# An output projection's bias: from a two-row product on the matrix engine to an add on GpSimd, in a fused embedding, state-space and mixture-of-experts kernel

## The reference

```python
def _L0_attn_ref(x, ...):
    ...                                            # u: projections, gate, convolution
    _, ys = jax.lax.scan(step, init, ...)          # state-space recurrence
    y = jnp.transpose(ys, (1, 0, 2))
    out = jnp.einsum('blh,dh->bld', y, W_out) + b_out
    return _layernorm(x + out, ln_g, ln_b)
...
h = tokens                                          # embedding of patches and text
h = h + _L0_attn_ref(_layernorm(h), ...)
h = h + _L0_ffn_ref(_layernorm(h), ...)             # router, top 2 of 4 experts, combined
```

## Time and profile before

| | us |
|---|---|
| three runs | 497.41, 498.78, 499.92 |
| median | 498.78 |
| span of the profiled execution, first to last instruction | 495.2 |
| busy in it: PE, DVE, ACT, POOL | 442.5, 330.5, 296.4, 152.2 |

### The profile page before, as it was taken

The page is one execution under the profiler, slowest core; times in us unless marked ns, Lnnn a source line. Parts: engine busy times, 40 slices in busy tenths (PEclk is TensorE's granted clock), DMA queues, the critical chain, the costliest instruction groups (busy, mean ns, idle before and its releaser), DMA issues.

```text
span 495.2 us, 9980 instructions
## 1 busy us (share of the span) xinstructions
PE 442.5 (89%) x3149; PEld 363.4 (73%) x3149; DVE 330.5 (67%) x980; ACT 296.4 (60%) x667; POOL 152.2 (31%) x255
## 2 busy tenths in 40 slices
PE   8989989799899999999999798999999999999400
PEld 5769967667778878887777577888878888888300
DVE  6885567678999434335786777866674666666584
ACT  2854359177975465316554354887786777877341
POOL 2000000000000000001243887874778644543322
PEclk9999999799999999999999999999999999999955
DMA  7981089900019942972511222232322333252262
GB/s 178 187 228 56 33 253 322 292 0 2 1 35 259 217 114 58 228 228 81 180 54 52 89 94 77 86 97 66 107 98 76 107 107 110 74 155 69 78 213 82
DMA packets 58734, 59.94 MB, mean 121 GB/s; under 512 B 25368, under 2 KB 51260, under 8 KB 57404
## 3 DMA queue, kind: packets, MB, share of 16 engines
q1 hardware_dynamic: 54236, 48.68, 36.4%
q0 software_dynamic: 3552, 9.74, 5.3%
q10 hardware_dynamic: 896, 0.89, 0.6%
HBM read 34.50 MB, written 24.80 MB: 120 GB/s over the span
## 4 chain that ended last, share of the span: by engine, by line
PE 66%; DVE 12%; issue 7%; ACT 7%; POOL 4%; DMA 2%; SPq 1%; DVEq 0%; POOLq 0%; ACTq 0%
PE bank L1040 14%; PE bank L881 9%; PE bank L433 8%; PE bank L435 8%; PE bank L434 8%; PE bank L955 3%; PE bank L1030 3%; PE bank L901 3%; POOL sorted_x L671 2%; PE bank L1012 2%; ACT U L470 1%; DVE spj L1400 1%; DMA got<-expert_y 1%; PE bank L848 1%; PE bank L947 1%
## 5 line engine op out<-in xcount | busy, mean ns | idle before, releaser
L1040 PE MATMUL bank<-w,hr 128*128 x320 | 76.0, 380 | 1.5 <-DVE ysb L1661 1.5
L1040 PEld LDWEIGHTS bank<-w,hr 128*128 128x128 f32 x320 | 60.1, 190 | 11.7 <-issue 2.7
L644 POOL MEMSET ones<- 2x128 f32 x1 | 0.2, 194 | 212.3 <-PE bank L916 212.3
L1234 ACT ACTIVATE hr<-bank,gsel 128x128 f32<-128x128 f32 x160 | 59.9, 460 | 0.2 <-PE bank L1030 0.2
L719 POOL DMA_INDIRECT expert_y<-ysb,toid x40 | 42.8, 1071 | 51.3 <-DVE ysb L1661 34.7
L881 PE MATMUL bank<-Tb,U 68*32 68x68 f32 x1024 | 45.9, 358 | 0.3 <-issue 0.3
L881 PEld LDWEIGHTS bank<-Tb,U 68*32 68x32 f32 x1024 | 40.6, 139 | 3.6 <-issue 3.1
L1646 DVE BATCH_NORM_STATS2 bsth<-bank 128x6 f32<-128x512 f32 x40 | 27.7, 693 | 20.5 <-PE bank L435 20.2
L671 POOL DMA_INDIRECT sorted_x<-x2s,slot x34 | 33.8, 994 | 15.3 <-issue 9.2
L1226 ACT ACTIVATE hn<-bank,nmrh,rsh 128x512 f32<-128x512 f32 x40 | 31.1, 777 | 10.0 <-DVE nmrh L1655 8.1
L433 PE MATMUL bank<-w_hi,bT_hi 128*128 x80 | 35.0, 438 | 0.1
(11 more groups left out here) (297 smaller groups left out, 1153.3 us busy)
## 6 DMA issues: line engine op xcount, KB each, us to landing
Tb<-ssm_kernels SPq DMA_DIRECT2D x16, 680.0 KB, 7.5
sorted_x<-zpad SPq DMA_DIRECT2D x6, 1419.0 KB, 13.6
xg<-sorted_x SPq DMA_DIRECT2D x40, 129.0 KB, 2.1
got<-expert_y SPq DMA_DIRECT2D x17, 256.0 KB, 3.6
XI<-in_x_dram SPq DMA_DIRECT2D x12, 288.0 KB, 5.6
h0r<-h_spill SPq DMA_DIRECT2D x17, 128.0 KB, 2.1
out_dram<-acc SPq DMA_DIRECT2D x17, 128.0 KB
w1raw<-in_L_ffn_w_dram SPq DMA_DIRECT2D x4, 512.0 KB, 15.9
```

The source lines that it names most:

```text
L1040: mm = pe.matmul(bank[6][:, 0:D], hr[:, i % 3, c, :], w2[:, bass.ds(expert[i], 1), c, :].rearrange("p o n -> p (o n)"), start=(c == 0), st ...
L1234: last = act.activation(hr[:, i % 3, c, :], bank[3 + i % 2][:, c * P:(c + 1) * P], ACT.Relu, scale=gsel[:, i, 0, c:c + 1], bias=gsel[:, i, ...
```

## The change

The bias is no longer a product. One DMA brings it to all 128 partitions (`bo`), POOL adds it to `xb` in the step `h0b`, ahead of the add that was there, and DVE's sum waits for POOL's semaphore `xb_bias` instead of ACT's `xb`. The product L959, its operands and the instructions that made them are gone. The planned times and so the order of steps on each engine are as before.

```diff
-        bo = zjunk[0:2, 1, :]
+        bo = zjunk[:, 1, :]
...
-                    for n in range(2):
-                        sp.dma_start(bo[n:n + 1, :], ins["L0_attn_b_out"].rearrange("(o d) -> o d", o=1)).then_inc(sem("small_in"), 16)
+                    sp.dma_start(bo, ins["L0_attn_b_out"].partition_broadcast(P)).then_inc(sem("small_in"), 16)
...
                 if kind == "h0b":
                     pool.wait_ge(sem("xb"), i + 1)
-                    pool.wait_ge(sem("small_in"), 80)
+                    pool.wait_ge(sem("small_in"), 144)
+                    pool.tensor_tensor(xb[:, i % 3, :], xb[:, i % 3, :], bo, ALU.add).then_inc(sem("xb_bias"), 1)
                     pool.tensor_tensor(h0r[:, i % 4, :], h0r[:, i % 4, :], lnb_b[:], ALU.add).then_inc(sem("h0b"), 1)
...
                     for j in range(HC):
-                        pe.matmul(ps, yT[:, i % 2, j, :], Wo[:, j, :], start=(j == 0), stop=False)
-                    if i == 0:
-                        pe.wait_ge(sem("router"), 2 + 2 * DC)
-                        pe.wait_ge(sem("block_consts"), 1)
-                    pe.matmul(ps, ones2[:], bo_hl[:], start=False, stop=True).then_inc(sem("out_mm"), 1)
+                        mm = pe.matmul(ps, yT[:, i % 2, j, :], Wo[:, j, :], start=(j == 0), stop=(j == HC - 1))
+                    mm.then_inc(sem("out_mm"), 1)
...
-                    dve.wait_ge(sem("small_in"), 160)
-                    dve.wait_ge(sem("sort_consts"), 10)
-                    link(dve.tensor_copy(bo_hl[:], bo))
-                    link(dve.tensor_tensor(bo, bo, bo_hl[:].bitcast(F32), ALU.subtract))
-                    link(dve.tensor_scalar(bo, bo, mB[:], None, ALU.mult))
-                    dve.scalar_tensor_tensor(bo_hl[:], bo_hl[:].bitcast(F32), mA[:], bo, ALU.mult, ALU.add).then_inc(
-                        sem("router"), 1)
...
                 if kind == "out":
                     dve.wait_ge(sem("out_mm"), i + 1)
-                    dve.wait_ge(sem("xb"), i + 1)
+                    dve.wait_ge(sem("xb_bias"), i + 1)
```

More of the change, by code:

```diff
@@ L141, in build_kernel @@
         rsum = sb("rsum", [P, NT])
-        mA = sb("mA", [2, 1])
-        mB = sb("mB", [2, 1])
         slot = sb("slot", [P, NT, 2], U32)
@@ L223, in build_kernel @@
         (hr,) = place(R5, R6, ("hr", [P, 3, HC, P]))
-        (bo_hl,) = place(AUX + size(HC, D) + size(2, D), R3, ("bo_hl", [2, D], F32R))
         (xT2,) = place(R6, R7, ("xT2", [P, DC, P]))
         (zpad,) = place(R6 + size(H), R7, ("zpad", [P, DX]))
-        ones2, ebk = place(R6 + size(H), R7, ("ones2", [2, P], F32R), ("ebk", [P, NK]))
+        (ebk,) = place(R6 + size(H), R7, ("ebk", [P, NK]))
         (busy,) = place(R6, R7, ("busy", [P, 512], F32R))
@@ L617, in _ @@
             pool.memset(tri[:], 1.0).then_inc(sem("sort_consts"), 1)
-            pool.memset(mA[:], 1.0).then_inc(sem("sort_consts"), 1)
-            pool.memset(mB[:], 0.0).then_inc(sem("sort_consts"), 1)
-            pool.wait_ge(sem("sort_consts"), 7)
+            pool.wait_ge(sem("sort_consts"), 5)
             pool.affine_select(out=tri[:], in_=tri[:], compare_op=ALU.is_gt, fill=0.0, base=0, pattern=[[1, P]],
[L622 to L625, removed]
                                channel_multiplier=-1).then_inc(sem("sort_consts"), 1)
@@ L643, in _ @@
             pool.wait_ge(sem("xs_zeroed"), 16 * FILLS)
-            pool.memset(ones2[:].bitcast(F32), 1.0).then_inc(sem("block_consts"), 1)
             pool.iota(kth[:], pattern=[[1, TAB]], base=0, channel_multiplier=0,
@@ L647, in _ @@
             pool.memset(before[:], 1.0).then_inc(sem("block_consts"), 1)
-            pool.wait_ge(sem("block_consts"), 3)
+            pool.wait_ge(sem("block_consts"), 2)
             pool.affine_select(out=before[:], in_=before[:], compare_op=ALU.is_gt, fill=0.0, base=0,
@@ L659, in _ @@
                       allow_small_or_imprecise_dtypes=True).then_inc(sem("block_consts"), 1)
-            pool.wait_ge(sem("block_consts"), 8)
+            pool.wait_ge(sem("block_consts"), 7)
             for kind, i in order("pool"):
@@ L903, in _ @@
                 elif step[0] == "wo":
-                    pe.wait_ge(sem("small_in"), 160)
+                    pe.wait_ge(sem("small_in"), 144)
                     for n in range(2):
@@ L987, in _ @@
                     if i == 0:
-                        pe.wait_ge(sem("sort_consts"), 10)
+                        pe.wait_ge(sem("sort_consts"), 6)
                     own = chosen[:, ts.start:ts.stop, :].rearrange("p t e -> p (t e)")
@@ L1553, in _ @@
                     if i == 0:
-                        dve.wait_ge(sem("block_consts"), 4)
+                        dve.wait_ge(sem("block_consts"), 3)
                     own = lg[:, ts, :].rearrange("p t (e o) -> p t e o", o=1).broadcast_to([P, w, E, E])
@@ L1574, in _ @@
                     if i == 0:
-                        dve.wait_ge(sem("sort_consts"), 10)
-                        dve.wait_ge(sem("block_consts"), 6)
+                        dve.wait_ge(sem("sort_consts"), 6)
+                        dve.wait_ge(sem("block_consts"), 5)
                     for n in range(w):
@@ L1591, in _ @@
                     if i == 0:
-                        dve.wait_ge(sem("block_consts"), 2)
+                        dve.wait_ge(sem("block_consts"), 1)
                     else:
```

## The result

The changed kernel took 523.16 us (median of 4 runs, 521.94 to 524.94) against 498.1 us before (4 runs, 497.25 to 499.92): ratio 1.0514, interval 1.0476 to 1.0553. The change makes the kernel 5.1% slower. The forecast was 521.5 with a range of 513 to 528. The profiled execution has a span of 521.0 us, 25.8 more than before, and took 522.8 us itself, so 1.8 us lie around the span.

What follows compares the result with a forecast made beforehand. The tile loop's path ran through PE, and any delay of the blocks delayed the end. After 2.0 us gained early, POOL-order stalls at tiles 10 to 16 left 23.2: 495.2 + 23.2 + 3.6 = 522.0, put at 521.5, range 513 to 528.

Steps and rivals of the forecast that it cites:

- rounded up: Final step: 522.0 us lowered to 521.5, because the hand-over added to each POOL bias add (0.8 us to `r1`) was rounded up.
- here 2.0 gained, nothing added: Tiles 0 to 9: removed PE bias products gain 2.0 us (bounds 1.0 and 2.8); the POOL add costs nothing.
- POOL sits idle until `xb` comes, nothing here: Tiles 0 to 9: POOL's add starts at once, covered by the tile's eight products, 1.9 us, so no cost.
- Rival 2: Tiles 0 to 9: POOL's adds slow DVE up to 0.5 us each for eight tiles; 2.0 lost, 526; chance 0.1.
- The step of 7.7 us: From tile 13's to tile 14's `r1`: two filler groups, transposes and products on PE at full clock, 7.7 us, giving 314.4.
- PE cold about 6.5: Tile 13's `r1`: PE at half clock takes about 6.5 us beside DVE's chain of 5.7, giving 306.7.
- The 314.4: POOL's `h0b` 14 ends at 314.4, then tables and block ids 6.5 and 0.8 us lead to tile 15's `r1` at 321.7.
- rival 1: PE's clock doesn't fall or returns at once: tile 11 1.9 us earlier, tiles 13 and 14 2.3; 517.8; chance 0.2.
- nothing later gives it back: Block stage: PE stands at 9 tenths until shortly before the end, so any delay of the blocks delays the end equally.
- (3): Stalls at tiles 10 and 12 overlap earlier waits, so the first block is 11.5 us late, not 16.8; 510.3; chance 0.1.
- (4): POOL reaches each bias add before PE ends the tile's products; only removed products count: 496.0, at most 493.5; chance 0.03.
- (5): Nothing measurable: stall and saving cancel, needing a stall of 3 us instead of the first 6.2; chance 0.02.

Runs made afterwards that it cites:

- e1_wait_only: Kernel before, with DVE's sum also waiting for POOL's `h0b` of its tile; bias still a product on PE, no second POOL add: 523.86 us, ratio 1.0495.
- e6_pool_from_10: Changed kernel's POOL bias add in `h0b` for tiles 10 to 16 only, tiles 0 to 9 keeping the kernel before's PE product: 522.2 us, ratio 1.0492.
- the placed versions: Changed kernel with bias adds of tiles 10 to 16 earlier in POOL's order: 505.02 us; variants with `h1b` behind blocks 3 to 11 or 17 to 25: 502.79, 497.54.
- table of `h1b` versions: Tile 0's to tile 9's sum, bias on POOL: 34.0 to 34.8 us with POOL's `onb_b` adds (`h1b`) in the loop, 30.8 to 32.1 without; on PE 32.4 to 32.5.
- e4_warm: Changed kernel with more filler products on PE in its three longest waits for DVE, results unused, to keep the clock up: 521.08 us, ratio 1.0463.
- e3_moved: Changed kernel with the bias adds of tiles 10 to 16 taken out of `h0b` and placed earlier in POOL's order: 505.02 us, ratio 1.0147.
- e10_h1b_later: Kernel before, with only POOL's `h1b` adds moved from the tile loop to behind blocks 17 to 25; bias still a PE product: 496.87 us, ratio 0.9979.
- e11_moved_later: Changed kernel with bias adds of tiles 10 to 16 earlier in POOL's order and `h1b` behind blocks 17 to 25: 497.54 us, ratio 1.0001.
- e12_to_9_later: Kernel before, with the bias of tiles 0 to 9 on POOL, the rest as PE products, and `h1b` behind blocks 17 to 25: 495.18 us, ratio 0.9939.

## Why the prediction was right, and which steps were off

**The mechanism.** Right, and shown by `e1_wait_only` (the wait alone has the whole loss), by `e6_pool_from_10` (it is at tiles 10 to 16) and by the placed versions (moving the adds in POOL's order removes seven tenths of it, and with `h1b` moved as well all that the runs can tell). The two long waits came out at 9.11 and 9.74 us, DVE's sum waits for POOL for 30.0 us where the forecast had 25 to 35, and the longest are those of tiles 10, 12 and 16.

**The terms of the sum.** Start times; the last column says how much the error against the forecast grew or shrank with this term.

| | before | forecast | after | error, change |
|---|---|---|---|---|
| scatters of tiles 0 to 3 | 268.37 | 266.4 | 269.46 | +3.1, +3.1 |
| `r1` of tile 10 | 272.59 | 278.75 | 281.76 | +3.0, -0.1 |
| `r1` of tile 11 | 276.85 | 284.6 | 287.87 | +3.3, +0.3 |
| scatters of tiles 4 to 7 | 281.60 | 287.9 | 291.18 | +3.3, 0 |
| `r1` of tile 12 | 284.05 | 300.2 | 303.45 | +3.3, 0 |
| `r1` of tile 13 | 289.75 | 306.7 | 309.57 | +2.9, -0.4 |
| `r1` of tile 14 | 297.64 | 314.4 | 315.87 | +1.5, -1.4 |
| `b1` of block 0 | 300.56 | 317.3 | 318.77 | +1.5, 0 |
| `r1` of tile 15 | 303.01 | 321.7 | 323.02 | +1.3, -0.2 |
| `r1` of tile 16 | 312.67 | 336.9 | 338.19 | +1.3, 0 |
| `b1` of block 5 | 317.32 | 340.0 | 340.71 | +0.7, -0.6 |
| end of span | 495.2 | 518.4 | 521.0 | +2.6, +1.9 |

The durations of POOL's queue, taken from rows (10.1 us of scatters, 1.4 of `h1b`, 0.8 to the sum), hold within 0.1 us at both stalls. Other terms were off and in part cancelled, so that the total came within 2 us is luck in part: the forecast ran 3.1 us early up to the first scatters and 1.9 behind block 5, 2.6 late between tile 12's sum and block 5, and 1.8 too long around the span. The 0.5 us taken off at the end, because the hand-over was "rounded up", was not due: it measured 0.80.

**The early gain.** The step "here 2.0 gained, nothing added" failed, by 3.1 us: the gain became a loss of 1.1 (1.7 from tile 0's sum to tile 9's, 0.65 less at tile 0). From tile 0's sum to tile 6's the removed products did save 1.1 us (16.2 against 17.3), not the 1.9 of six products: at tiles 1, 4 and 6 the sum waits last for POOL's add (1.89, 0.97 and 0.99 us), so the add was not wholly covered even there. And "POOL sits idle until `xb` comes, nothing here" looked only at whether the add is hidden, not at whom it holds up while it runs. Rival 2 named this, gave it 0.1 and a smooth price of 0.5 us per tile. What happened is a single chain at tiles 7 and 8: a run of adds, DVE held, PE idle 2.62 us, clock at 0.50. The argument against the rival, that the adds fall into DVE's waits, holds for the tiles up to 6 only. The table of `h1b` versions shows that it takes the `h1b` adds as well, which together with the bias make such runs. It is rival 2's mechanism added to the forecast, not in its place.

**Tile 14.** The step of 7.7 us took 6.3. PE's work in it was sized rightly: two groups of fillers, the transposes and the products took 7.5 us from 307.99, and tile 14's sum waited 0.42 us for them. What failed is where they begin. The forecast had PE end tile 13's products with tile 13's sum ("PE cold about 6.5", at half clock), and added the 7.7 to that sum. But the granted clock was back at 307, some 3 us after PE resumed at 303.93, so PE ended them and began the fillers at 307.99, 1.6 us ahead of tile 13's sum, which waited for DVE's own chain. In `e6_pool_from_10`, with the same instructions there, the clock was back only some 5 us after PE resumed, and the step is 7.4 us; in `e4_warm` it is 5.9. The 314.4 at which the forecast lets POOL's `h0b` 14 end, and the 2.3 us of rival 1 for tiles 13 and 14, are worked out from no row; it ended at 315.8.

**The blocks.** The forecast let everything behind block 5 shift as one. From block 5 to 6 the step was 6.3 us instead of 4.6, since PE had waited 2.3 us for DVE's `slot` and 2.13 us for `bT_lo` ahead of it, and the clock was at 0.50 at 342. That is 1.7 us, for which the sum had 0.5. From block 6 on the shift stays at 25.1 to 25.2 (321.92 to 347.00) until the last block, as forecast: nothing later gives it back. Behind the last block another 0.6 us is added, which I have no reason for.

**Around the span.** I took 3.6 us from the median less the span; the profiled execution after had 1.8 (`e3_moved` 504.9 - 503.0 = 1.9, `e10_h1b_later` 497.1 - 495.4 = 1.7). The median and the span of another execution don't make that number. It hid 1.8 of the 2.6 us that the span was short.

**The rivals.** (1) was tested by `e4_warm`: the clock does fall, and keeping it up returns about 2 us, half of the rival's 4.2. (2) was right in sign and at tiles 7 and 8 alone, as said. (3), a partial absorption, did not occur: block 0 came 18.2 us later, not 11.5. Nor did (4), the faster case, or (5), no change: the wait at tile 10 was 9.11 us, where (4) needs it near nothing and (5) 3 us. The conditions of (4), POOL free by 271.8 through another order, were set up in `e11_moved_later`, and even there the ratio is 1.0001: a gain of 2.8 us in the whole kernel was not to be had.

**What stays open.** In `e3_moved` 6.6 us stayed lost. The 6.58 us pair is 5.7 longer than 0.88, but the step it lies in grew only by 2.8 us (10.7 against 7.9), the next by 2.4, and how the rest is divided was not separated. Of `e12_to_9_later`'s 0.6%, `e10_h1b_later` (the same `h1b`, the product kept) has 0.2% and the bias the rest, 1.7 us by the medians; the two intervals just touch (0.9919 to 0.9958 and 0.9958 to 1.0001), so the bias's share is small and not sharply known. What else in its later tiles makes `e11_moved_later` slower than `e10_h1b_later`, beside the step to tile 12, was not separated. And why a DVE instruction outlasts a whole run of POOL's adds in `e3_moved` and `e11_moved_later`, and only single adds elsewhere, is open.

## What to carry to other kernels

Moving a step onto an engine that is mostly idle costs what stands ahead of it in that engine's order, not its own duration: here 0.73 us per add became 9 to 10 us twice. Read the place in the order before the busy share, and when a cheap step feeds an early user, give it a place of its own instead of merging it into a step that was placed for a late one. Then look at what the added instructions do to the neighbour that shares an interface with them: count the length of the resulting runs, not the instructions. And before work is moved out of the way, look at the queue it is moved into: the same `h1b` adds cost 0.8% at blocks 3 to 11 and nothing that the runs can tell at blocks 17 to 25 (there the trace gives back 0.9 us of the 2 us gained in the tile loop).

## What the runs showed of the hardware

The hold-up of DVE by POOL has no fixed price. A pair of 128x256 `SCALAR_TENSOR_TENSOR` with both tensor inputs in SBUF took 0.88 us alone, 1.34 to 1.82 beside POOL adds, 3.31 us beside three adds back to back (`e11_moved_later`) and 6.58 us beside eight (`e3_moved`). In these last two one DVE instruction, begun 0.5 and 0.4 us ahead of the first add, ended 0.3 us behind the last. A 128x2 `TENSOR_TENSOR` went from 0.15 to 0.70 us, about one POOL add. DVE's sum, with one input in PSUM and one in SBUF, was 402 to 425 ns in all 17 cases after the change. The Trainium skill, SBUF — State Buffer, "Who interferes with whom", has the pair of ports shared by DVE and GpSimd as an exclusive lock that whoever starts first holds for its whole instruction, and says that only DVE instructions with two SBUF inputs or in a two-port mode contend for it. The traces agree on who contends, and the 0.70 us is one POOL add long. The 6.58 and 3.31 us are not: there DVE's instruction, the first to start by the profile, outlasted a whole run of adds and not one.

The clock came back after very different times. PE resumed at 282.24 and the granted clock was 1.00 again in the window at 290; it resumed at 303.93 and was at 1.00 in the window at 308. Both waits had been 9 us long. A wait of only 2.62 us at 256.48 was also followed by 0.50, in all windows from 256 to 262 (3.62 us for eight products).
